# Sending both attentions' score rows through DRAM value by value, and reordering the filling of a four-layer graph kernel

## The reference, cut to what matters

```python
# layer 1 ("A" in the kernel) and layer 3 ("C")
Wh = h @ W                                     # per graph 1024 x 128
s, t = Wh @ a_src, Wh @ a_dst
e = leaky_relu(s[:, :, None] + t[:, None, :], 0.2)
e = where(adj == 0, -inf, e)                   # layer 3: a very negative number
out = softmax(e, axis=-1) @ Wh                 # layer 3: elu(...) of it
# layer 2 ("B")
e = leaky_relu((h * a_0) @ h.T, 0.2)           # kept where adj == 1
out = softmax(where(adj == 1, e, -9e15)) @ h
```

## Time and profile before

| what | before |
| --- | --- |
| median of 3 runs | 1531.18 us (1531.07 to 1531.24) |
| the profiled execution: its own time, its span | 1534.19 us, 1532.4 us |
| mean granted share of TensorE's clock in it | 0.963 |
| busy: PE, DVE, ACT, POOL | 92%, 74%, 54%, 25% of the span |
| the pipeline's steps: filling, then a steady step | 440 to 634 us, then about 62 us each |

### The profile page before, as it was taken

The page is one execution under the profiler, slowest core; times in us unless marked ns, Lnnn a source line. Parts: engine busy times, 40 slices in busy tenths (PEclk is TensorE's granted clock), DMA queues, the critical chain, the costliest instruction groups (busy, mean ns, idle before and its releaser), DMA issues.

```text
span 1532.4 us, 33041 instructions
## 1 busy us (share of the span) xinstructions
PE 1402.3 (92%) x12740; PEld 1269.2 (83%) x12740; DVE 1133.6 (74%) x3270; ACT 826.6 (54%) x1825; POOL 380.9 (25%) x337
## 2 busy tenths in 40 slices
PE   5899999799946679999999999999999999999886
PEld 5899999555536469999999998989999999999786
DVE  4566665687834667888888888888888888887565
ACT  4687778022232455746656566556574665655521
POOL 6334340000010214133132231331313313232120
PEclk9899999799968789999999999999999999999998
DMA  9999992376741122231431313313223143131111
GB/s 206 225 199 206 211 212 69 103 252 233 247 152 45 52 77 76 56 90 38 109 90 50 97 47 93 104 36 104 72 74 90 36 110 90 36 83 22 49 42 43
DMA packets 109599, 161.95 MB, mean 106 GB/s; under 512 B 9472, under 2 KB 61312, under 8 KB 107392
## 3 DMA queue, kind: packets, MB, share of 16 engines
q1 hardware_dynamic: 85248, 117.86, 26.7%
q0 software_dynamic: 19584, 33.56, 11.9%
q10 hardware_dynamic: 4608, 8.39, 1.6%
HBM read 151.40 MB, written 41.94 MB: 126 GB/s over the span
## 4 chain that ended last, share of the span: by engine, by line
PE 44%; DVE 13%; ACT 6%; DVEq 3%; POOL 2%; issue 2%; DMA 0%; ACTq 0%
PE ps L1598 27%; PE ps L1557 4%; DVE wts_A L946 3%; PE ps L1580 3%; PE ps L1532 2%; PE ps L1569 2%; POOL rs_C L851 2%; DVE wts_C L946 2%; PE ps L1571 2%; PE ps L1570 2%; ACT hN L1279 1%; ACT hV L1276 1%; PE ps L1541 1%; DVEq L979 1%; DVE st_C L884 1%
## 5 line engine op out<-in xcount | busy, mean ns | idle before, releaser
L1598 PE MATMUL ps<-hP_A,wts_A 128*128 128x129 f32 x2112 | 255.3, 276 | 3.7 <-DVE wts_A L946 3.0
L862 POOL TENSOR_TENSOR wts_B<-wts_B,off 128x1024 f32<-128x1024 f32 (+7 forms) x128 | 174.5, 1388 | 335.8 <-PE ps L1580 335.8
L1598 PE MATMUL ps<-hV,wts_B 128*128 128x129 f32 x2048 | 246.5, 276 | 4.4 <-DVE wts_B L961 2.6
L1598 PEld LDWEIGHTS ps<-hP_A,wts_A 128*128 128x128 f32 x2112 | 245.3, 192 | 5.0 <-DVE wts_A L946 4.0
L1598 PEld LDWEIGHTS ps<-hV,wts_B 128*128 128x128 f32 x2048 | 238.8, 193 | 5.3 <-issue 3.0
L1598 PE MATMUL ps<-hP_C,wts_C 128*128 128x129 f32 x1920 | 220.1, 274 | 0.0
L1598 PEld LDWEIGHTS ps<-hP_C,wts_C 128*128 128x128 f32 x1920 | 217.4, 191 | 0.5
L946 DVE SCALAR_TENSOR_TENSOR wts_A<-row_A,least_A,ring_A 128x1024 f32<-128x1024 f32 x128 | 160.8, 1274 | 7.5 <-ACT row_A L1304 4.7
L294 ACT ACTIVATE maskT<-ps 128x1024 fp8e4<-128x1024 bf16 x128 | 131.2, 1025 | 59.5 <-PE ps L336 48.2
L946 DVE SCALAR_TENSOR_TENSOR wts_C<-row_C,least_C,ring_C 128x1024 f32<-128x1024 f32 x120 | 160.2, 1346 | 0.0
L348 PE MATMUL ps<-x,adj_b 128*128 128x129 f16 x896 | 122.4, 225 | 16.1 <-ACT whn L277 13.1
(11 more groups left out here) (234 smaller groups left out, 2694.7 us busy)
## 6 DMA issues: line engine op xcount, KB each, us to landing
adj_b<-in_adj POOLq DMA_DIRECT2D x120, 256.0 KB, 9.8
maskT_scratch<-maskT SPq DMA_DIRECT2D x16, 1024.0 KB, 6.9
ring_A<-maskT_scratch SPq DMA_DIRECT2D x64, 256.0 KB, 3.1
off<-maskT_scratch SPq DMA_DIRECT2D x32, 512.0 KB, 6.4
ring_C<-maskT_scratch SPq DMA_DIRECT2D x64, 256.0 KB, 3.3
xa<-in_x SPq DMA_DIRECT2D x16, 512.0 KB, 4.5
whT_scratch<-whT_s ACTq DMA_DIRECT2D x32, 256.0 KB, 6.5
whT_b<-whT_scratch SPq DMA_DIRECT2D x16, 512.0 KB, 4.8
```

What stands on the lines that cost most here:

```text
L862: pool.tensor_tensor(w, w, off_fp8[:, k, k * P:N], ALU.mult).then_inc(S["B", "up"], 1)
L1598: last = nc.tensor.matmul(Q_SLOTS[c // 2 % 2][:, c % 2, 0:PW], wts[y][:, j, c * P:c * P + P], src[:, j, :], start=(j == 0), stop=(j == T - 1))
```

## The change

1. **The rows.** For A of graphs 3 to 15 and C of graphs 0 to 13 (`VIA`), PE's `rows` and ACT's `row_power` are gone. ACT takes the exponential of `us` itself (128 x 8) and issues a DMA (`store_row`) that writes the 1024 values one by one, 4 bytes each, into a row of 4 KB in DRAM; SP then loads that row into all 128 partitions of `row_A` or `row_C` (`load_row`, 512 KB written to SBUF). `load_row` for C stands on SP ahead of `load_q` and the last mask loads of C, for A behind `load_x` and ahead of `save` and the next mask loads. DVE's first weight waits for this load.
2. **The weights of A.** Where A's row comes by DRAM, the weights 0, 1 and 2 of A's next graph move on DVE from ahead of B's last shares to behind the moments of C's norm.
3. **The ELU's second half**, `elu_negative`, moves on DVE from after `lower(6)` to after the last weight of C, in the same steps.
4. **The filling.** A of graphs 0, 1 and 2 uses `weigh_half`. For graphs 1 and 2 (`EARLY`) it stands ahead of `gram`, at the step's start, and all eight weights of these graphs are made in the step before; the `shares` and `scaled` of the first two pairs move with it. In step 2 `turn_h("C")` moves behind the first `gram`.

The diff, cut:

```diff
+        row_dram = {x: nc.dram_tensor(f"row_scratch_{x}", (2, T, P), fp32).ap() for x in "AC"}
...
+            us_e = {x: a_rep[:, 0, k * T:(k + 1) * T] for k, x in enumerate(cases)}
+            VIA = {"A": range(3, B), "C": range(0, B - 2)}
...
+            EARLY = (1, 2)
...
+                    def load_row(x, b):
+                        n = b - VIA[x].start
+                        sp.wait_ge(S[x, "s_out"], (n + 1) * 16)
+                        if b > 0:
+                            sp.wait_ge(S[x, "wts"], b * T)
+                        sp.dma_start(row_e[x][:, :], row_dram[x][n % 2].rearrange("t p -> (t p)").partition_broadcast(P)) \
+                            .then_inc(S[x, "s_in"], 16)
...
                             load_mask("A", i + 1, 1)
+                        if i - 2 in VIA["C"]:
+                            load_row("C", i - 2)
                         if 1 <= i + 2 < B:
                             load_q(i + 2)
...
                             load_x(i + 2)
+                        if i + 1 in VIA["A"]:
+                            load_row("A", i + 1)
                         if 0 <= i - 3:
                             save(i - 3)
...
-                            dve.wait_ge(S[x, "s_row"], 2 * b + 2)
+                            if b in VIA[x]:
+                                dve.wait_ge(S[x, "s_in"], (b - VIA[x].start + 1) * 16)
+                            else:
+                                dve.wait_ge(S[x, "s_row"], 2 * turned_rows(x, b) + 2)
...
+                        if i == 0 or i in EARLY:
+                            shares("A", i, 0)
+                            shares("A", i, 1)
...
-                        if post and GW:
+                        if post and GW and i + 1 not in VIA["A"]:
                             elu_negative(i - 3)
...
+                        if i == 1:
+                            weights("A", 2, 0)
+                            lowest("A", 2)
+                            weights("A", 2, 1)
                         if GW:
                             add("B", i - 1, 0, newC, oldC)
+                        if i == 1:
+                            weights("A", 2, 2)
+                            weights("A", 2, 3)
...
-                        if nextA:
+                        if post and GW and i + 1 in VIA["A"]:
+                            elu_negative(i - 3)
+                        if nextA and i != 1 and i + 1 not in VIA["A"]:
                             weights("A", i + 1, 0)
...
+                        if i == 0:
+                            for j in range(2, T):
+                                weights("A", 1, j)
+                        if i == 1:
+                            for j in range(4, T):
+                                weights("A", 2, j)
-                        if nextA:
+                        if nextA and i + 1 not in EARLY and i + 1 not in VIA["A"]:
                             weights("A", i + 1, 2)
...
                             moments("C")
-                        if nextA:
+                        if i + 1 in VIA["A"]:
+                            weights("A", i + 1, 0)
+                            lowest("A", i + 1)
+                            weights("A", i + 1, 1)
+                            weights("A", i + 1, 2)
+                        if nextA and i + 1 not in EARLY:
                             weights("A", i + 1, 3)
...
+                    def store_row(x, b):
+                        n = b - VIA[x].start
+                        act.wait_ge(S[x, "us"], b + 1)
+                        if n > 0:
+                            act.wait_ge(S[x, "s_out"], n * 16)
+                        nc.scalar.activation(us_e[x], us[x][:, :], ACT.Exp, scale=1.0 - SLOPE).then_inc(S[x, "s_kept"], 1)
+                        act.wait_ge(S[x, "s_kept"], n + 1)
+                        if n > 1:
+                            act.wait_ge(S[x, "s_in"], (n - 1) * 16)
+                        act.dma_start(row_dram[x][n % 2].rearrange("t p -> p t"), us_e[x], allow_slow_non_contiguous=True) \
+                            .then_inc(S[x, "s_out"], 16)
...
-                        if CA:
-                            row_power("C", i - 2, 0)
+                        if CA and i - 2 in VIA["C"]:
+                            store_row("C", i - 2)
...
                             scaled("B", i - 1, 0)
+                        if i + 1 in VIA["A"]:
+                            store_row("A", i + 1)
                         if AA:
                             normed("B", i, newB, 0)
...
+                        if i in EARLY:
+                            weigh_half("A", i)
+                        if CA and i != 2:
                             turn_h("C", i - 2, hN, free_q, 0, "hT")
...
-                                if j == 4:
-                                    rows("C", i - 2, free_q, 0)
...
                             turn_h("A", 1, hN, free_p, 1, "hT")
-                        for c in range(T):
+                            weigh_half("A", 0)
+                            values("A", 1, free_p, 0, T)
+                        c0 = T // 2 if 0 <= i <= 2 else 0
+                        for c in range(c0, T):
                             if AA:
                                 weigh("A", i, c)
...
-                            if c == 0 and CA and AA:
-                                rows("C", i - 2, free_q, 1)
...
-                                if c in (4, 5):
+                                if c in (4, 5) and i + 1 not in VIA["A"]:
                                     rows("A", i + 1, free_p, c - 4)
```

More of the change, by code:

```diff
@@ L760, in gnn_stack_kernel @@
             S["C", "quo_exp"] = csem("C_quo_exp")
+            for x in cases:
+                for n in ("s_kept", "s_out", "s_in"):
+                    S[x, n] = csem(f"{x}_{n}")
             for n in ("var", "rstd", "shift", "h", "hT_made", "ahi", "lo", "gram", "kept", "lrelu", "exps", "turned", "low", "up", "tile", "rec", "quo", "done"):
@@ L1096, in run @@
                             shares("C", i - 3, 3)
-                        if AA:
+                        if AA and i not in EARLY:
                             weights("A", i, 7)
+                        if i == 0 or i in EARLY:
+                            shares("A", i, 0)
+                            shares("A", i, 1)
                         if GW:
@@ L1138, in run @@
                             stats("A", newA, 0)
-                        if AA:
+                        if AA and i > 2:
                             shares("A", i, 0)
@@ L1413, in run @@
                             scaled("C", i - 3, 3)
+                        if i == 2:
+                            scaled("A", i, 0)
+                            scaled("A", i, 1)
+                            keep_scores(i - 1, 0)
                         if CA:
@@ L1416, in run @@
                         if GW:
-                            keep_scores(i - 1, 0)
+                            if i != 2:
+                                keep_scores(i - 1, 0)
+                            if i == 1:
+                                scaled("A", i, 0)
+                                scaled("A", i, 1)
                             keep_scores(i - 1, 1)
@@ L1443, in run @@
                         if AA:
-                            scaled("A", i, 0)
-                            scaled("A", i, 1)
+                            if i not in EARLY:
+                                scaled("A", i, 0)
+                                scaled("A", i, 1)
+                            scaled("A", i, 2)
                             if i == 0:
@@ L1448, in run @@
                                 row_power("A", 1, 1)
-                            scaled("A", i, 2)
                         if nextA and i != 0:
@@ L1471, in run @@
                             exps("A", i + 1)
-                        if nextA and i != 0:
+                        if nextA and i != 0 and i + 1 not in VIA["A"]:
                             row_power("A", i + 1, 0)
@@ L1535, in rows @@
                     def rows(x, b, free, h):
-                        take(free, 1, S[x, "s_row"], 2 * b + h + 1)
+                        take(free, 1, S[x, "s_row"], 2 * turned_rows(x, b) + h + 1)
                         if h == 0:
@@ L1664, in run @@
                             if CA:
+                                if i == 2 and j == 0:
+                                    turn_h("C", i - 2, hN, free_q, 0, "hT")
                                 if j == 1:
@@ L1680, in run @@
                             if i == 0:
[L1681 to L1683 removed]
+                                if c == 4:
                                     highest("A", 1, free_p, 1)
[L1685 to L1687 removed]
+                                if c in (5, 6):
+                                    rows("A", 1, free_p, c - 5)
+                            if c == c0 and nextA and i > 0:
                                 turn_q(i + 1)
[L1689 to L1692 removed]
```

(4 more changed lines are left out.)

15 lines of the change are left out of this document (3 added, 12 removed).

## The result

The changed kernel takes 1563.27 us (median of four runs, 1561.31 to 1565.07) where the kernel before takes 1531.12 beside it: a ratio of 1.0201 (1.0188 to 1.0214), 2% slower. The forecast was 1530.8 with a range to 1548: wrong. What happened is the second rival, the row that lands late, which had a chance of 0.13 and a price that came to 1557, though the row that is late is another than the one priced.

A forecast was written before the change was run, and what follows sets the result against it. PE's list was taken to bound steps 3 to 14, a chain of DVE, ACT and POOL the filling. Terms −6.7 + 0.9 + 5.8 − 0.4 = −0.4 us turned 1531.18 into 1530.8 us, range 1508 to 1548.

The forecast's parts named there:

- the second rival: A's row lands late at DVE's first weight, 2.0 us in 13 steps: slower, 1557 us; chance 0.13.
- the price of the row's way: Rows through DRAM, store plus load: bounded by 6.3 to 15.4 us, taken as 7 us with no wait.
- my own case: The forecast's case, gains and losses of 6 us cancelling, each perhaps off by half: 1523 to 1538 us; chance 0.38.
- The moved weights: Steady step on DVE, A's weights behind C's moments: `turn_h("C")` 1.80 us later after W, PE about 2.0 us idle.
- W: The start of C's weighings on PE in a steady step, predicted to come 1.32 us earlier.
- What PE is spared: Steady step on PE: transposes and a wait for DVE gone, less an ACT delay; C's weighings start 1.32 us earlier.
- C's first group: C's first group of transposes, inside B's scores where PE waits for ACT anyway: counted as nothing.
- The filling: Steps 0 to 2, before the steady pattern: B's weighings in step 2 come 6.7 us earlier, kept in the sum.
- the fourth rival: The filling's 6.7 us is given back when step 3's pattern sets in: 1537 us; no separate chance, counted in the forecast.
- The clock rival: PE's clock falls in the new gap ahead of `turn_h("C")`: 1551 us, or 1541 in half the steps; chance 0.17.

The follow-up runs named there:

- wide: The changed kernel with PE transposing the 128 x 8 values to 8 x 128, so each row is stored in 8 pieces of 512 bytes: 1555.38 us, 1.0144.
- wide_late: wide with the store of A's row moved behind the first half of B's norm on ACT: 1538.38 us, 1.0035.
- fill_move: The changed kernel with all rows still made by PE and ACT, so the filling and the DVE moves alone: 1552.25 us, 1.0130.
- c_wide: The kernel before with the filling and C's rows through DRAM in pieces of 512 bytes, A's rows by PE, no DVE moves: 1526.87 us, 0.9957.
- fill_only: The changed kernel with all rows by PE and ACT and no weights or ELU moved, the filling alone: 1530.24 us, 0.9989.
- c_on_pe: The changed kernel with C's rows made by PE and ACT as before, A's still through DRAM: 1571.57 us, 1.0259.
- rot_both: The changed kernel with A's weights 0 to 2 put behind C's third shares, the others in the next step: 1581.22 us, 1.0317.

## Why the prediction was wrong

1. **The step that failed is the price of the row's way**: "I take a value near the lower end, 7 us, and nothing for the wait". It was 9.65 + 4.2 = 13.9 for C and 7.95 + 4.7 = 12.7 for A in step 8. I had bounded it by 6.3 to 15.4 and argued from `out`, whose pieces are as many but 512 bytes long, that a store alone in its queue would be near the fastest. `wide` refutes that: queue and place are the same there, and 8 pieces instead of 1024 take 1.2 us. I had misread `out` too: it is one store of 512 KB per graph, not two halves behind other stores, and its three stores at the kernel's end landed in 3.2 to 3.6, so its minimum told of pieces of 512 bytes and of no others. With the slow store gone the whole change takes 1538.38 (`wide_late`), the upper end of my own case's 1523 to 1538.
2. **Whom the late row hits was wrong too.** I had A late at the moments, 2.0 in 13 steps. It was C, 54.5 us of DVE's idle time against 8.5 for A: C's budget of 10.7 us is the shorter and its store the longer. At the 13.6 that I priced, C would have been 2.9 late by that budget, and I did not count it. The second rival's 1557 came near the result by a wrong distribution.
3. The Trainium skill, "DMA: Bandwidth & Descriptors" (Rules for kernel authors), spoke against this store, and I weighed it too low. Its rule, one descriptor per element where the last dimension is not contiguous, agrees with the trace: ACT's queue (q10 of the page) has 32688 − 4608 = 28080 packets more than before, 27 stores of 1040.
4. **The moved weights**: right. +1.80 from W to `turn_h("C")` was predicted, +1.9 measured (`fill_move`), 2.0 us of PE's idle time predicted, 1.67 measured.
5. **What PE is spared**: right in sum, 1.32 predicted, 1.36 in step 8 of `wide_late`, 1.10 as the mean. The single terms were not measured, and that they agree so well in sum is in part luck: C's first group was not free of effect, as PE then waits 0.46 more among the scores, and in `c_wide`, where only C's two groups are gone, the first part is no more than 0.04 shorter.
6. **The filling** failed as a term of the sum. The lead was there where I worked it out, 8.1 us at the start of B's weighings in step 2 for the 6.7 predicted, but the sum let it last, and in `fill_only` nothing of it is left at step 3 (193.6 for 193.5). That is the fourth rival, which I had counted in the forecast's own range; its 1537, 6 over the kernel before, is close to `wide_late`, 5.3 over it. In the changed kernel step 3 begins 4.2 later than before, 1.4 of it by the moves; the first late row of C falls into step 2, where PE waits 8.03 us.
7. **The clock rival** did not come true. PE's gap was 1.67 us, shorter than the 2.0 that I worked out, and with it in each step the granted clock is 1.00 in step 8.

The two costs don't add up. Alone, over the filling, the move costs 22 us and C's late row 22; A's late row adds 19 to the move. All together with PE's gain they make 32 over the kernel before. One part of this is seen: A's row is late 8.5 us beside C's late row and 24.3 without it, as its store is 1.2 us shorter there. Why C's late row costs the first part 1.75 alone and only 0.42 beside the move (46.42 against 46.00 in `c_on_pe`) is not shown. So undoing C's part alone makes it worse (`c_on_pe`), and making both rows' stores short takes 25 us off (`wide`'s edit in `wide_late`).

## What to carry to other kernels

When a value is sent round through DRAM, price it by its pieces and not by its bytes: a transpose of 0.11 us on PE (996.89 to 997.00 in `wide`) that makes 8 pieces of 512 bytes of 1024 pieces of 4 saved 5.5 to 9.7 us of latency per row. `wide` changes the number and the size of the pieces together; but `out` has 1024 pieces of 512 bytes and landed in 3.2 to 3.6 us at the kernel's end, which speaks against the number alone. Ask of a late transfer what is queued behind the waiting instruction: here it was not the weights but the shares behind them that held PE. And idle time of an engine is no room by itself: three weights of 1.2 us cost 1.7 us per step ahead of C's norm, and made PE wait 3.15 behind it, on an engine that is idle 9 us in each step.

## What was not expected of the hardware

From the store's issue on ACT to the load's issue on SP, 1024 pieces of 4 bytes took 6.7 to 11.0 us, 8 pieces of 512 bytes 1.2. The DMA engines were not busy for it. The page's third part, for ACT's queue after, against 1.6% before:

```profile
q10 hardware_dynamic: 32688, 8.50, 2.4%
```

The 0.8% more are 0.008 × 16 × 1560 = 200 us of engine time, 7.4 us per store, under half a microsecond on each of 16 engines. The packets are also through early. For C's store of step 8, issued at 965.97, the DMA view of 965.9 to 968.5 and that of 968.5 to 975.6, where the load is about to be issued, give:

```profile
DMA packets 1041, 0.02 MB, mean 8 GB/s; under 512 B 1040, under 2 KB 1040, under 8 KB 1040
...
DMA packets 0, 0.00 MB, mean 0 GB/s; under 512 B 0, under 2 KB 0, under 8 KB 0
```

All of the store's 1040 packets lie in the first 2.5 us, and in the 7.1 us up to the load's issue the core has no DMA packet at all. In all 27 stores the last packet ended within 4.0 us of the issue. So here the time passes neither in moving the values nor behind other transfers. Nor is it SP's list: SP issues nothing in between, and the load goes out 0.01 to 0.23 us after the last update of the store's semaphore. What holds that update back for 1024 pieces of 4 bytes and not for 8 of 512, no row shows. Of PE's clock: with idle times of 1.67 us in every step the granted clock was at full (1.00 in step 8), and behind those of 3.15 us in `rot_both` it was lower (16 matmuls in 3.33 us, 0.97 over the step).
